# Attention with FFN on one core: key and query copies moved from GpSimd to DMA, and both rounding remainders given to GpSimd

## The reference

```python
xn = layernorm(x)
c_q, c_kv = xn @ Wq_down, xn @ Wkv_down                 # latent size 64
q_c, k_c, v_c = up-projections of c_q, c_kv             # 128 heads of 4
q_r = (xn @ Wq_rope).reshape(b, s, 128, 64)             # 64 per head
k_r = xn @ Wk_rope                                      # 64, shared by all heads
scores = (q_c . k_c + q_r . k_r) / sqrt(68)
s = softmax(scores) @ v_c @ Wo
g = silu(ffn(xn))                                       # gate/up/down with low-rank parts
out = x + s * g
```

## Time and profile before

| what | value |
|---|---|
| median of 3 runs | 2336.41 us (2326.87 to 2337.11) |
| the profiled execution | 2331.98 us, its span 2330.2 us |
| PE busy (matmul records) | 1974.4 us, 85% of the span |
| PEld, DVE | 1537.0 us (66%), 1630.3 us (70%) |
| ACT, POOL | 1493.7 us (64%), 1456.7 us (63%) |
| granted TensorE clock, mean | 0.944 |
| DMA moved | 124.53 MB, mean 53 GB/s |

### The profile page before, as it was taken

The page is one execution under the profiler, slowest core; times in us unless marked ns, Lnnn a source line. Parts: engine busy times, 40 slices in busy tenths (PEclk is TensorE's granted clock), DMA queues, the critical chain, the costliest instruction groups (busy, mean ns, idle before and its releaser), DMA issues.

```text
span 2330.2 us, 41105 instructions
## 1 busy us (share of the span) xinstructions
PE 1974.4 (85%) x12538; PEld 1537.0 (66%) x12538; DVE 1630.3 (70%) x1626; ACT 1493.7 (64%) x2000; POOL 1456.7 (63%) x1692
## 2 busy tenths in 40 slices
PE   8988888888888888788888888888888888887899
PEld 7766666666666666666666666666666666765666
DVE  8666777676777767677767777676767676665664
ACT  6566666766667767677666777676676766644222
POOL 5456576766667666767676776667675767523443
PEclk9999999999999999999999999999999999988899
DMA  7411111111111121111111111111111111224542
GB/s 251 140 28 41 30 47 28 35 32 37 38 35 34 25 48 28 46 29 36 32 38 38 35 35 26 46 29 47 28 35 31 38 38 37 46 71 133 162 136 68
DMA packets 145576, 124.53 MB, mean 53 GB/s; under 512 B 51518, under 2 KB 105566, under 8 KB 145502
## 3 DMA queue, kind: packets, MB, share of 16 engines
q1 hardware_dynamic: 145478, 123.87, 21.3%
q10 hardware_dynamic: 48, 0.03, 0.0%
HBM read 61.26 MB, written 35.65 MB: 42 GB/s over the span
## 4 chain that ended last, share of the span: by engine, by line
issue 24%; PE 23%; DMA 16%; SPq 13%; POOL 11%; ACT 6%; DVE 5%; POOLq 1%; ACTq 0%; DVEq 0%
PE st L1118 11%; DMA slot<-mrow 10%; SPq L784 6%; PE ob L1152 3%; SPq L739 3%; DVE mx L1027 3%; DMA w_stage<-in_Wq_rope 3%; PE sx L1133 2%; POOL k L830 2%; POOL slot L850 2%; POOL vb L886 2%; SPq L735 2%; PE ob L1084 2%; ACT pf L1000 2%; ACT pw L1008 1%
## 5 line engine op out<-in xcount | busy, mean ns | idle before, releaser
L1027 DVE TENSOR_REDUCE mx<-sx 128x4 fp32r<-128x1024 f32 x512 | 624.8, 1220 | 226.8 <-PE sx L1133 224.4
L1118 PE MATMUL st<-slot,k 128*128 128x512 f32 x1024 | 448.7, 438 | 183.1 <-DMA slot<-mrow 156.3
L1000 ACT ACTIVATE pf<-st 128x1024 f32<-128x1024 f32 x464 | 451.6, 1015 | 175.3 <-PE st L1118 173.4
L853 POOL TENSOR_TENSOR pw<-pf,pw 128x1024 f16<-128x1024 f32 x232 | 510.5, 2200 | 47.6 <-ACT pw L1008 47.6
L1052 DVE TENSOR_TENSOR pw<-pf,pw 128x1024 f16<-128x1024 f32 x232 | 398.5, 1718 | 173.4 <-ACT pw L1008 171.6
L830 POOL CAST k<-kc 64x512 fp32r<-64x512 f32 x256 | 170.1, 664 | 536.4 <-PE st L1118 536.2
L1008 ACT ACTIVATE pw<-pf 128x1024 f16<-128x1024 f32 x464 | 464.2, 1051 | 16.0 <-PE ob L1084 14.4
L1118 PE MATMUL st<-slot,krlh 128*128 128x512 f32 x1024 | 433.6, 423 | 0.0
L1133 PEld LDWEIGHTS sx<-k,slot 88*128 88x128 f32 x2048 | 317.6, 198 | 133.4 <-issue 89.7
L1133 PE MATMUL sx<-k,slot 88*128 88x256 f32 x2048 | 350.4, 295 | 51.7 <-DMA slot<-kx 34.5
L1118 PEld LDWEIGHTS st<-slot,k 128*128 128x128 f32 x1024 | 210.5, 206 | 252.1 <-issue 209.9
(11 more groups left out here) (246 smaller groups left out, 2774.2 us busy)
## 6 DMA issues: line engine op xcount, KB each, us to landing
w_stage<-in_Wq_rope SPq DMA_DIRECT2D x64, 256.0 KB, 4.6
o_scratch<-o_sb SPq DMA_DIRECT2D x256, 64.0 KB
c_scratch<-stage SPq DMA_DIRECT2D x32, 256.0 KB, 3.0
c_in<-c_scratch SPq DMA_DIRECT2D x128, 64.0 KB, 2.0
k<-kc SPq DMA_DIRECT2D x128, 48.0 KB
k<-kx SPq DMA_DIRECT2D x128, 48.0 KB
slot<-kx SPq DMA_DIRECT2D x256, 24.0 KB
slot<-kc SPq DMA_DIRECT2D x255, 24.0 KB
```

The source lines that it names most:

```text
L853: nc.gpsimd.tensor_tensor(pw[:, s, 0, 1], pf[:, 2 * (k % 2)], pw[:, s, 0, 0], ALU.subtract).then_inc(lo_done[0], 1)
L1000: nc.scalar.activation(dst, st[:, kt], ACT.Exp, scale=SCALE).then_inc(exp_done, 1)
L1027: nc.vector.tensor_reduce(mx[:, p, lo:lo + 4], sx[:, :, :].rearrange("p a (b k) -> p (a b) k", b=2), axis=AX.X, op=ALU.max).then_inc(red_d ...
L1118: last = nc.tensor.matmul(st[:, kt, h, :].rearrange("p (e n) -> p e n", e=PH), kk, q[:, s, :, h, :], start=(n == 0), stop=(n == 1))
```

## The change

- The copy of the rope keys into `k1[0:64]` becomes a DMA (64 partitions of 2 KB) that SP issues first in `load_content`, counted by `ct_in`, whose final count rises from 48 to 64 a turn. `k_ready` goes away; SP waits for `st_done` of the step four back itself.
- The copy of the rounded queries into `slot2[0:64]` becomes a DMA (64 partitions of 4 KB) that SP issues at the end of the next step's loads (`copy_queries`), with a semaphore `s2_in` for each slot.
- POOL computes both remainders; DVE's one is gone. DVE takes the second maxima of a step at the end of the same body instead of at the start of the next.
- The output stores move from place 2 (step k-7) to place 1 (step k-6) in SP's order.
- Some waits of POOL ahead of the content copies, and places of three small memsets in the last stage, follow from this.

The diff, cut to what the steps need:

```diff
         def load_content(sp, at, k, heads=PH):
             if not at.live(k - NS):
                 sp.wait_ge(slot_zeroed, s + 1)
                 sp.wait_ge(k1_filled, s + 1)
-            if k > 1 or not at.first:
-                hold(sp, passed, k_ready, u + 1)
+            else:
+                hold(sp, passed, st_done, 2 * u - 6)
+            sp.dma_start(k1[0:64, s, :, :].rearrange("p a n -> p (a n)").bitcast(F32),
+                         krh[:, bp * CH:(bp + 1) * CH].bitcast(F32)).then_inc(ct_in[s], 16)
...
+            def copy_queries(at, k):
+                s = k % NS
+                hold(sp, passed, qh_done, 2 * at.step(k) + 2)
+                sp.dma_start(slot2[0:64, s].rearrange("p e a n -> p (e a n)").bitcast(F32),
+                             slot1[0:64, s].rearrange("p e a n -> p (e a n)").bitcast(F32)).then_inc(s2_in[s], 16)
...
+                if at.live(k - 1) and k <= STEPS:
+                    copy_queries(at, k - 1)
...
-                elif k % NS == 2 and at.live(k - 7):
-                    store_o(at, k - 7)
+                elif k % NS == 1 and at.live(k - 6):
+                    store_o(at, k - 6)
...
-                    nc.gpsimd.tensor_copy(k1[0:64, s, :, :].rearrange("p a n -> p (a n)"),
-                                          krh[:, bp * CH:(bp + 1) * CH]).then_inc(k_ready, 1)
...
                     if s == 2 and at.live(k + 2):
-                        hold(pool, passed, k_ready, u + 1)
+                        if at.live(k - NS):
+                            hold(pool, passed, st_done, 2 * u - 6)
...
-                if at.live(k - 1) and k <= STEPS:
-                    hold(pool, passed, qh_done, 2 * u)
-                    nc.gpsimd.tensor_copy(slot2[0:64, (k - 1) % NS], slot1[0:64, (k - 1) % NS]).then_inc(s2_done, 1)
                 if at.live(k - 4) and at.split(k - 4):
-                    hold(pool, passed, hi_done, 2 * at.parts(k - 4) - 1)
-                    nc.gpsimd.tensor_tensor(pw[:, s, 0, 1], pf[:, 2 * (k % 2)], pw[:, s, 0, 0],
-                                            ALU.subtract).then_inc(lo_done[0], 1)
+                    for kt in range(2):
+                        hold(pool, passed, hi_done[kt], at.parts(k - 4))
+                        nc.gpsimd.tensor_tensor(pw[:, s, kt, 1], pf[:, 2 * (k % 2) + kt], pw[:, s, kt, 0],
+                                                ALU.subtract).then_inc(lo_done[kt], 1)
...
             def body(at, k):
-                if at.live(k - 2) and k - 2 < STEPS:
-                    maxima(at, k - 2, 1)
...
+                    for half in range(2):
+                        maxima(at, k - 1, half)
...
-                if at.live(k - 4) and at.split(k - 4):
-                    dve.wait_ge(hi_done, 2 * at.parts(k - 4))
-                    nc.vector.tensor_tensor(pw[:, k % NS, 1, 1], pf[:, 2 * (k % 2) + 1], pw[:, k % NS, 1, 0],
-                                            ALU.subtract).then_inc(lo_done[1], 1)
```

More of the change, by code:

```diff
@@ L79, in __init__ @@
         self.o_stored = sem("o_stored")
-        self.k_ready = sem("k_ready")
         self.ql_done = sem("ql_done")
@@ L665, in attention @@
         ql_done = at_sems.ql_done
-        s2_done = sem("s2_done")
-        k_ready = at_sems.k_ready
+        s2_in = [sem(f"s2_in{s}") for s in range(NS)]
         ct_in = at_sems.ct_in
@@ L676, in attention @@
         exp_done = sem("exp_done")
-        hi_done = sem("hi_done")
+        hi_done = [sem(f"hi_done{kt}") for kt in range(2)]
         lo_done = [sem(f"lo_done{kt}") for kt in range(2)]
@@ L725, in load_content @@
         def load_content(sp, at, k, heads=PH):
-            s, u = k % NS, at.step(k)
+            s, u, bp = k % NS, at.step(k), (k // NS) % NBP
             c = content[(k // NS) % 2]
@@ L837, in body @@
                     if s == 2 and at.live(k + 2):
-                        hold(pool, passed, k_ready, u + 1)
+                        if at.live(k - NS):
+                            hold(pool, passed, st_done, 2 * u - 6)
+                        if at.live(k - 5):
+                            if at.split(k - 5):
+                                hold(pool, passed, lo_done[1], at.parts(k - 5))
+                            else:
+                                hold(pool, passed, vx_ready, u - 4)
+                        if k == 14 and not at.last:
+                            hold(pool, passed, w_ready, NS * at.g + NS + 1)
                         copies(k // NS + 1, at.turn(k) + 1)
@@ L1007, in rounded @@
                     act.wait_ge(exp_done, 2 * v + kt + 1)
-                    nc.scalar.activation(pw[:, k % NS, kt, 0], pf[:, 2 * (k % 2) + kt], ACT.Copy).then_inc(hi_done, 1)
+                    nc.scalar.activation(pw[:, k % NS, kt, 0], pf[:, 2 * (k % 2) + kt], ACT.Copy).then_inc(hi_done[kt], 1)
             def refill(g, s):
@@ L1039, in body @@
                                                 slot1[0:64, s, e, :, :], ALU.subtract).then_inc(ql_done, 1)
-                    if k % NS:
-                        maxima(at, k - 1, 0)
                     if k % NS == 0:
@@ L1106, in scores @@
                 if kt == 0:
-                    pe.wait_ge(s2_done, v + 1)
+                    pe.wait_ge(s2_in[s], 16 * (at.turn(k) + 1))
                 if kt == 0 and k % 2 == 0:
@@ L1127, in row_scores @@
                     pe.wait_ge(qh_done, 2 * v + 2)
-                    pe.wait_ge(ct_in[s], 48 * (at.turn(k) + 1))
-                    if at.first and k < 2:
-                        pe.wait_ge(k_ready, k + 1)
+                    pe.wait_ge(ct_in[s], 64 * (at.turn(k) + 1))
                 for h in range(2):
@@ L1427, in sync_tail @@
             for landed in at_sems.ct_in:
-                sp.wait_ge(landed, 48 * NT)
+                sp.wait_ge(landed, 64 * NT)
             for row in (0, 32):
@@ L1432, in sync_tail @@
             sp.wait_ge(at_sems.mrow_in[1], 16 * NT)
-            sp.wait_ge(at_sems.k_ready, NS * NT)
             sp.wait_ge(at_sems.o_stored, 64 * (NT - 2))
@@ L1489, in pool_tail @@
     def pool_tail(pool, k):
-        if k == 1:
+        if k == 0:
             pool.wait_ge(at_sems.w_ready, NS * G2)
@@ L1499, in pool_tail @@
             nc.gpsimd.memset(a2[:, :, :, :], 0.0).then_inc(ab2_zero, 1)
-        if k == 9:
+        if k == 10:
             nc.gpsimd.memset(b2_raw, 0.0).then_inc(ab2_zero, 1)
@@ L1555, in act_tail @@
                 act.wait_ge(b2_loaded, 16 * 4)
-                act.wait_ge(at_sems.k_ready, NS * NT)
+                for landed in at_sems.ct_in:
+                    act.wait_ge(landed, 64 * NT)
                 nc.scalar.activation(hh[:, 0, :], b2_raw, ACT.Copy, scale=0.5).then_inc(b2_hi, 1)
```

5 lines of the change are left out of this document (removed).

## The result

The changed kernel takes 2240.36 us (median of 4 runs, 2215.9 to 2245.73) against 2334.35 us (4 runs, 2326.87 to 2337.11): a ratio of 0.958, 95% interval 0.950 to 0.966. It is faster, by 94 us, where 254 were forecast, and lies above the range of 1990 to 2200. The profiled execution took 2235.8 us, with a span of 2234.0.

The account below looks back on a forecast made before the run. PE was taken to lose time to two latency chains, the maxima row's DMA and DVE's maxima. -156 - 90 - 29 - 95 + 46 + 44 + 26 = -254 on 2332.0 gave 2078, as median 2082 us; range 1990 to 2200.

Parts of the forecast that it names:

- The step that failed: At place 2, content DMAs issued at 5.4 us and landing in 2.3 arrive 7.1 in, ahead of place 3's row scores.
- the part on DMA copies: SP's queue: 30 issues a turn instead of 22, busy 22 of 26 us; the copies' DMAs arrive in time.
- Cover 0.5 us: Content of place 2: there 7.1 us in, wanted at 5.6 + 2.0 for the row scores of place 3.
- Content late: SP's issues or content landings take longer, at place 2: 87 us, up to 99 more for the clock; 2170 to 2270, chance 0.12.
- SP's queue is behind at place 2: Sign that the forecast would be wrong on the slow side; no size given.
- Stores moved: Stores at place 1 let the maxima row go out early at place 3; PE's whole 156.3 us wait goes.
- VectorE's remainder removed: Without DVE's remainder of kt 1 the maxima precede PE's transpose; 90.1 us of waits go.
- the 29: Each of 171 removed PE waits costs 0.17 us more than its counted idle time: 29 us.
- Clock: PE's clock no longer falls after the long wait: 56 x 1.7 = 95 us gained, mean clock 0.98 or more.
- GpSimd: POOL's two remainders at 2.15 us each leave no slack; values wait 0.8 us a turn, nearly 3 once a group.
- The sum: All terms together: -254 us on the profiled 2332.0, so 2078, or 2082 us as median.

Follow-up runs that it names:

- the two fastest kernels: Changed kernel with stores cut 32 partitions first instead of pair member first: 1991.67 us; the same with stores at place 3: 1986.67 us.
- the first group: Among others, changed kernel with the rope copy back on GpSimd, 2165.19 us, or the query copy back on GpSimd, 2137.66 us.

## Why the prediction was wrong

- **The step that failed** is the arrival of the content of place 2 in the part on DMA copies: "stores end at about 2.65 us into it, its issues at 5.4, and with a landing of 2.3 after the last one starts it is there 7.1 in", with "Cover 0.5 us". In the stretch shown it was there 11.0 us in (1027.41), 3.9 late. The landing is 2.8 of that: 5.13 us, not 2.3. The issue is the other 1.1: it started 5.9 in, not 4.8. PE was ready 7.7 in, as forecast (7.6). 3.9 less the cover is 3.4; PE waited 3.47.
- **Where the 2.3 came from:** a DMA of the preamble (`krlh`), with no slow stores just ahead of it. Content without slow stores just ahead lands in 2.5 to 2.8 us at the median of each place. The row that showed the rest was in my hands: the earlier trace rows has the maxima row landing 5.05 us after its issue, directly behind the same stores. I read that as a property of that place, used it for the row that left it, and gave the content that came to stand there the undisturbed price. The slowing moves with the stores, to whatever stands behind them.
- **The rival was right** in place and size. "Content late" priced just this landing, 87 us and up to 99 for the clock, 2170 to 2270 us; it had the wait at 2.3 us, without the late issue. What I held against it, a mean DMA share of 0.19, says nothing when one transfer has two packets in flight. The sign "SP's queue is behind at place 2" was right too.
- **Stores moved:** right for the row that left; all 156 us are gone, and more came in their place. Alone, in the kernel before, the move gives 90 us.
- **VectorE's remainder removed:** right in mechanism, too small. Without the wake it is worth 247 us, where I had 90 and some 20 of the 29. I had only counted the idle time ahead of the transposes; row scores wait for maxima too, and the instruction itself gets longer when GpSimd subtracts beside it.
- **Clock:** wrong as it came out (0.922), since falls follow the new waits of 3 to 4 us. In the two fastest kernels it is 0.981, as I had it for "no long wait left".
- **GpSimd:** right. Its remainder took 2.14 us (I: 2.15; the Trainium skill's factor of about two, "GPSIMD Engine Reference", "Performance versus the Vector engine", would give 2.46, an estimate, and this trace does not agree). My addition of its cycle was off: the terms give 25.95 us, not 25.7 (and the planes 3.92, not 3.95), still level with PE's 25.8. With the delay gone, the new wait at the values is 0.83 us in an ordinary turn and 2.63 once a group; forecast 0.8 and nearly 3. GpSimd is then busy for 84% of 600 to 1500 us. Returning a copy to GpSimd costs 88 and 111 us, so it has no slack.
- **The sum** was too small a gain even without the failed step: it gave 2082, and the two kernels without the wake take 1992 and 1987. A turn there takes 26.3 to 26.5 us (548 and 544 score matmuls `st<-slot,k` in 900 us at 16 a turn) against 31.9 before (452). 5.5 us over 64 turns is 350. My sum went by recorded waits of two kinds, where the same text's schedule of a turn (25.0 and 0.8) gave nearly the whole of it; the difference lay in it unread.

The Trainium skill has the mechanism: "DMA: Bandwidth & Descriptors", "Why a DMA increments its semaphore by 16 and not by 1", says that a DMA from SP runs on the largest number of engines up to 16 that divides the slowest dimension of both access patterns. For a leading dimension of 2 that is two, for 32 it is 16. The traces agree: a DMA share of 0.14 and two packets in flight with the old cut, 0.69 and up to 17 with the new one. Which of the engines carried them isn't in the trace and wasn't tried, and no cut between 2 and 32 was.

In the first group either copy's removal helped by 75 and 103 us, by different ways, as the table there shows. Without the rope copy's issue the content goes out 0.6 us sooner and lands no faster. Without the query copy it goes out as late and lands 1.0 us sooner, and the stores' packets pass in 6.4 us instead of 7.1, so the query copy's data do lengthen the wake. What stays open is how much of the 75 and 103 us each of these effects is.

## What to carry to other kernels

When a transfer is moved in a queue, ask what will stand behind it now, and give that the landing time of what stood behind it before, if it goes out as soon. Look at the DMA share while one transfer passes: here a low one with long landings behind was a transfer with few packets in flight. Cutting it along a dimension of 32 was worth more here than the whole change: 113 us in the kernel before, against 94. And weigh the parts of a change again after the bound has gone: beside the delay, all of the change but the move of the stores was worth nothing that the runs can tell (2244 and 2240), and with the new cut the two kernels lie 235 us apart (2227 and 1992, the stores at different places).

## What was not expected of the hardware

- Four 64 KB stores with a leading dimension of 2 pass at 29 to 41 GB/s and a DMA share of 0.12 to 0.14; with 32 in front the stretch that holds them shows 172 GB/s and 0.69 (the end of the query copy is in it), and the four issues take 2.25 us instead of 2.87.
- A DMA issued close behind the slow ones lands late: content of 24 KB issued 2.4 us after the stores' issues ended takes 4.9 us at the median instead of 2.7, the maxima row of 8 KB 5.05 instead of 1.8. Issued 3.9 us after them, the content takes 2.6.
- VectorE's float32 subtract takes 1.65 to 2.44 us where GpSimd's overlaps it, 2.02 in the mean of all, and 1.23 where it doesn't. GpSimd's own takes 2.15 us with or without it in that kernel; in the kernel before, the 28 that overlap VectorE's take 2.37 in the mean, up to 3.1, the other 84 take 2.15.
